# An attention pipeline with a lag of 11 slots in place of 13, and the softmax of a group in three slots in place of five

## What is computed

```
Xq = (H @ W_lin.T).reshape(bt, n, h, dh)
Xv = (H @ W_val.T).reshape(bt, n, h, dh)
Qs = Xq[:, src]
Kt = Xq[:, dst]
e = jnp.einsum('behd,hd->beh', jax.nn.leaky_relu(Qs + Kt, LRELU_SLOPE), a)
e = e + jnp.log(A0[src, dst] + EPS)[None, :, None]
...
attn = ex / denom[src]
Vt = Xv[:, dst].transpose(1, 0, 2, 3)
Y = jax.ops.segment_sum(attn[..., None] * Vt, src, num_segments=n)
...
x = _layernorm(x + _L1_gnn_ref(x, ...))
```

## Time and profile before

| | |
|---|---|
| median of 3 runs | 858.69 us (858.43 to 860.77) |
| the profiled execution | 858.85 us, its span on the core 856.9 us |
| granted TensorE clock, mean | 0.99 |
| PE, DVE, ACT, POOL busy | 822.7, 672.7, 602.1, 262.7 us |
| first weighting of a leaving tile (L1687) | at 662.6 us |
| last weighting of a leaving tile | at 842.2 us |

### The profile page before, as it was taken

The page is one execution under the profiler, slowest core; times in us unless marked ns, Lnnn a source line. Parts: engine busy times, 40 slices in busy tenths (PEclk is TensorE's granted clock), DMA queues, the critical chain, the costliest instruction groups (busy, mean ns, idle before and its releaser), DMA issues.

```text
span 856.9 us, 14362 instructions
## 1 busy us (share of the span) xinstructions
PE 822.7 (96%) x4882; PEld 704.7 (82%) x4882; DVE 672.7 (78%) x1492; ACT 602.1 (70%) x1061; POOL 262.7 (31%) x642
## 2 busy tenths in 40 slices
PE   8999999999999999999999999999999999999685
PEld 7888888878888878888887888878888998988674
DVE  6888888868888878777778677767867787887776
ACT  3778778886767867777666667566787778786345
POOL 0233333340000000000000000102677677777856
PEclk9999999999999999999999999999999999999888
DMA  5222221000000001000000077677248746544513
GB/s 150 63 67 62 63 62 50 2 1 1 2 0 1 1 1 50 1 0 1 1 1 1 0 172 172 147 178 166 99 126 266 232 135 204 173 161 152 176 59 95
DMA packets 37896, 70.55 MB, mean 82 GB/s; under 512 B 3360, under 2 KB 24512, under 8 KB 32704
## 3 DMA queue, kind: packets, MB, share of 16 engines
q0 software_dynamic: 4608, 33.56, 15.3%
q1 hardware_dynamic: 32288, 35.73, 13.3%
q10 hardware_dynamic: 928, 0.35, 0.2%
HBM read 36.06 MB, written 16.78 MB: 62 GB/s over the span
## 4 chain that ended last, share of the span: by engine, by line
PE 77%; POOL 7%; DVE 7%; ACT 4%; issue 3%; DMA 1%; POOLq 0%; DVEq 0%; ACTq 0%
PE psum L514 9%; PE psum L515 9%; PE psum L516 9%; PE psum L532 7%; PE psum L528 6%; PE psum L529 6%; PE psum L424 3%; PE psum L466 3%; PE psum L1406 3%; PE psum L401 2%; PE psum L399 2%; PE psum L400 2%; POOL rstd L1257 2%; PE psum L1329 2%; PE psum L1351 1%
## 5 line engine op out<-in xcount | busy, mean ns | idle before, releaser
L654 ACT ACTIVATE work<-psum,bias 128x512 f32<-128x512 f32 (+2 forms) x364 | 228.9, 666 | 35.8 <-PE psum L532 31.9
L514 PE MATMUL psum<-hT_hi,w_hi 128*128 128x512 f32 (+2 forms) x362 | 139.4, 385 | 1.2 <-ACT work L654 1.2
L515 PE MATMUL psum<-hT_lo,w_hi 128*128 128x512 f32 (+2 forms) x362 | 139.1, 384 | 0.0
L516 PE MATMUL psum<-hT_hi,w_lo 128*128 128x512 f32 (+2 forms) x362 | 138.8, 384 | 0.0
L635 ACT ACTIVATE work<-work 128x512 f32<-128x512 f32 (+1 forms) x100 | 61.3, 613 | 94.8 <-DVE work L977 58.6
L1218 POOL DMA_DIRECT2D hT_lo<-hT_hi x8 | 7.6, 947 | 339.8 <-DVE hT_lo L924 320.4
L988 DVE TENSOR_TENSOR work<-work 128x512 f32<-128x512 f32 (+1 forms) x99 | 66.6, 673 | 47.7 <-ACT work L635 47.7
L528 PE MATMUL psum<-hs_hi,w_hi 128*128 128x512 f32 (+2 forms) x256 | 98.2, 384 | 0.3 <-DVE hs_hi L922 0.3
L532 PE MATMUL psum<-hs_lo,w_hi 128*128 128x512 f32 (+2 forms) x256 | 98.4, 384 | 0.0
L529 PE MATMUL psum<-hs_hi,w_lo 128*128 128x512 f32 (+2 forms) x256 | 97.6, 381 | 0.0
L970 DVE TENSOR_TENSOR work<-work 128x512 f32<-128x512 f32 (+1 forms) x100 | 66.3, 663 | 20.7 <-ACT work L654 20.6
(11 more groups left out here) (234 smaller groups left out, 1888.6 us busy)
## 6 DMA issues: line engine op xcount, KB each, us to landing
work<-x_by_batch SPq DMA_DIRECT2D x32, 256.0 KB, 2.6
x_stage<-x_by_state SPq DMA_DIRECT2D x8, 1024.0 KB, 5.7
hT_lo<-hT_hi POOLq DMA_DIRECT2D x8, 1024.0 KB, 8.4
hT_lo<-x_stage POOLq DMA_DIRECT2D x8, 1024.0 KB, 7.2
v_rows<-values SPq DMA_DIRECT2D x32, 256.0 KB, 2.4
out<-x_kept SPq DMA_DIRECT2D x31, 256.0 KB, 2.4
work<-L_gnn_Wih SPq DMA_DIRECT2D x4, 256.0 KB, 3.0
work<-L_gnn_Whh SPq DMA_DIRECT2D x3, 256.0 KB, 3.2
```

The lines of the kernel that those rows point to most:

```text
L514: pe.matmul(out, w_hi[:, w, g, :], xh, start=True, stop=False)
L515: pe.matmul(out, w_hi[:, w, g, :], xl, start=False, stop=False)
L516: mm = pe.matmul(out, w_lo[:, w, g, :], xh, start=False, stop=(t == 0))
L654: op = act.activation(gate[s][g][:, 0:ph.width(tile)], psum[:, 4 * s + g, 0:ph.width(tile)], ACT.Tanh if g == G else ACT.Sigmoid, bias=bia ...
```

## The change

LAG becomes GT + 3 = 11, RING stays 26 tiles, and the nine steps of the softmax stand in three slots. The exponential stands in the second of them instead of the third. Everything else follows from LAG: slots 0 to 10 take tiles in, slots 11 to 31 do both, slots 32 to 43 bring tiles out; VectorE scales the queries of 11 tiles instead of 13; the late tiles are 21 to 31 instead of 19 to 31. The slots of `LATE_SUMS`, of the value fetches and of the last input load are numbers of their own and stay.

```
@@ -1031,8 +1031,8 @@
-    LAG = GT + 5
-    RING = LAG + 13
+    LAG = GT + 3
+    RING = LAG + 15
@@ -1164,7 +1164,8 @@
-    STEPS = (((0,), (1,)), ((2,), (3,)), ((4,), (5,)), ((6,), ()), ((7,), (8,)))
+    STEPS = (((0,), (1, 2, 3)), ((), (4, 5)), ((6, 7), (8,)))
+    EXP_PART = 1
@@ -1573,7 +1574,7 @@
             g, part = softmax_at(n)
-            if part == 2:
+            if part == EXP_PART:
                 exponentials(g)
```

## The result

| | before | after |
|---|---|---|
| median of 20 runs each, on the same chips | 859.31 us | 861.29 us |
| lowest and highest | 856.07 to 860.95 | 860.51 to 864.55 |
| profiled execution | 858.85, span 856.9 | 861.23, span 859.4 |
| granted TensorE clock, mean | 0.99 | 0.988 |

The ratio is 1.0023 by the medians and 1.0030 by the comparison of the runs, with a 95% interval of 1.0019 to 1.0041: the change costs 2 to 2.6 us, at the edge of what a measurement can tell. The time lies inside the predicted range of 855.6 to 861.9 and 2.6 us above the predicted 858.7.

What follows compares the result with a forecast made beforehand. TensorE was taken to bound the kernel through slot 31, then VectorE until the last softmax is out. Terms 5.36 - 6.22 - 0.72 + 0.90 + 0.50 = -0.18 on 858.85 gave 858.7 us, range 855.6 to 861.9.

Steps and rivals of the forecast that it cites:

- The two regimes: TensorE bounds the kernel until slot 31 ends, then VectorE until the last softmax is out; two leaving tiles move between them.
- 5.36 - 0.72: Slots 11 and 12 become double, +5.36 us; waits around the first leaving tile change by 0.55 + 0.85 - 2.12 = -0.72.
- the 1.41: TensorE's longest wait around the first leaving tile, held up by GpSimd's value fetches; 0 to 1.41 us expected in slot 12.
- Rival 5: Values of the first tiles arrive late; three us of lateness in slot 11 would give 861.7 us; chance 0.02.
- Slots 16 to 31: New TensorE waits: +0.90 us in slot 16 from GpSimd's DMA issues, +0.50 in group 1 from VectorE's moved steps.
- group 2: VectorE's lateness there runs into slot 28's existing 1.09 us wait: put at 0, at most 1.0 us.
- The tail term: Two tiles fewer inside the last softmax on VectorE, 3.11 us each, bring its product earlier by the whole 6.22 us.
- The signs: Product ends some 12 us behind first step; slot 32 about 6 later; waits in slots 9, 12, 16, 20, not 13.
- Rival 1: TensorE's clock doesn't fall after the 4.24 us hole in the tail, saving 3.2: 855.5 us; chance 0.12.
- Rivals 2 to 4: Number 4 here: one more scan holds GpSimd in each of groups 0, 1 and 2, 3 x 0.68: 860.7 us; chance 0.05.
- rival 2: VectorE and GpSimd become the bound during each softmax; all waits at upper bounds, together 3.2: 861.9 us; chance 0.18.
- rival 3: The new waits of 0.55, 0.85, 0.90 and 0.50 don't appear: 855.9 us; chance 0.08.

Runs made afterwards that it cites:

- Experiments 4: Changed kernel with the last group's two accumulating DMAs issued one slot later, in slots 15 and 19: 859.75 us, ratio 1.0000 to the kernel before.
- experiment 5: Changed kernel with each softmax's subtraction moved one slot later, ahead of that slot's weighting: 861.60 us, ratio 1.0025 to the kernel before.
- experiment 3: Both kernels with matmuls on constants filling the tail's TensorE holes: 856.87 us for the changed kernel, 855.92 for the one before.
- experiment 6: Both kernels with tile 22's output issued ahead of the last softmax's turning: 854.60 us for the changed kernel, 853.31 for the one before.

## Why the prediction was right, and where it was off

**The two regimes** held: the price is TensorE's, ahead of slot 32, the gain is VectorE's, behind it, and they nearly cancel. From slot 8's gather to the start of slot 16 it came out as forecast, +4.64 for 5.36 - 0.72, but by luck, with terms that err against each other: slot 9 waits 0.70 instead of 0.55, slot 12 not at all instead of 0.85, and the waits of 0.50 and 0.21, which I let go with the 1.41, only moved to slots 11 and 12. Rival 5 didn't occur: the first weighting waited for no DMA.

**Slots 16 to 31** were mis-sized: 1.40 forecast, 2.58 measured. By the starts of the slots, slot 16 grew by 1.37 (I took 0.90 between 0 and 1.56) and slot 17 by 0.76 (0.50); both are more than the waits of 1.05 and 0.43 that the timeline shows, since matmuls that start after a wait overlap with none before them (slot 16's gather, where it doesn't wait, begins 0.16 us before the matmuls ahead of it end). The rest is mostly group 2, which I put at 0: the lateness of slots 24 and 25 (+1.05) isn't swallowed by slot 28, whose wait shrinks by only 0.53. Experiments 4 and 5 confirm who is late: GpSimd in slot 16, VectorE's moved steps, for the most part, in 9, 17 and 25.

**The tail term** was right in mechanism and off in size: -4.59 instead of -6.22. The failing step is the sentence that TensorE has less to do than VectorE there "in either version, so the product, and all that follows it, comes earlier by the whole 6.22". In microseconds of work that is so. But the two scans and the subtraction that now stand ahead of VectorE's addition make TensorE wait for it, the clock falls in the work behind that hole, and at the lower level TensorE is late for VectorE's next addition. With the holes filled the term is 6.07 (experiment 3), and the product starts 11.67 us behind the first step; with the clock up by itself it is 5.94 (experiment 6).

**The signs** that the prediction named came out mixed. The product ends 13.58 us behind the first step, not some 12; slot 32 begins 7.16 later, not about 6. TensorE waits for the query's low part in slots 9, 16 and 20, not in 12, and not in 13. And one sign of being wrong came: from the start of slot 24 to the end of slot 28 the change adds 1.01 us, more than a turned softmax (0.65 in slot 19). That is the term of group 2, put at 0.

**Rival 1**, that the clock might not fall behind the hole ahead of the turning, didn't come: in all five profiles that have this hole at 4.2 us or more and unfilled, the sum behind it took 3.1 to 3.8 us. Behind shorter holes it is a matter of the single execution: 2.20 and 2.21 ahead of the sum of tile 22 (the result and experiment 6), and in experiment 5 the sum of tile 24 took 2.05 us behind the same hole of 3.20 behind which it took 3.47 to 3.78 elsewhere:

```profile
823.91 2.05 PE L1407 MATMUL psum<-from_node,values 128*128 128x128 f32 x16 [3.20 <-DVE values L1688]
```

That the Trainium skill, page TensorE: Matmul & The Clock Gate, section "Part 1: The HAM clock gate", calls the window free-running fits this; no run here moved that phase on purpose. **Rivals 2 to 4:** the time stands nearer to rival 2's 861.9 than to the forecast, but only 1.18 of its 3.2 us came about, in slots 16 to 31; of the waits that rival 3 leaves out, those of slots 9, 16 and 17 appeared and that of slot 12 didn't; and a scan's hold on GpSimd was seen again (a cast at 689.43 took 0.64 us beside the scan from 689.39) but not tried by itself.

Together the time lies inside the range because two terms that were off in the same direction stayed small: +1.18 in slots 16 to 31 and +1.63 in the tail, with -0.25 for the rest and what lies outside the span. These are the 2.56 between the forecast -0.18 and the 2.38 that the two profiled executions are apart.

## What to carry to other kernels

When work moves between engines, look not only at who is busier in each stretch, but at where the other engine will stand idle in the new order: an idle TensorE can be paid for again in the work that follows. When a schedule shifts, look also at the slots that were left as plain numbers: moving two DMA issues of GpSimd by one slot took away the change's whole loss. Before trading tiles between a stretch bound by one engine and a stretch bound by another, look there for an order that makes both wait for each other; here one output issued ahead of a transposition was worth 6.5 us, and the trade nothing. And where TensorE's clock falls in one version's holes, fill the holes of both with matmuls on constants and compare them so: what is left is the change itself.

## What the runs showed of the hardware

- Behind the same wait the clock fell in one execution and not in another. Behind a wait of 1.64 us in slot 20 the changed kernel ran on at 1.00; behind 1.65 us at the same place, in experiment 5, the clock was granted at 0.63 for four microseconds, and the stretch to slot 24's wait took 29.10 us instead of 27.51. The rows, of the changed kernel and of the kernel of experiment 5:

```profile
716.50:720.50 4.00, 3.91 (x33) 3.91 (x34) 3.05 (x10) 3.56 (x9) 3.31 (x8) 1.00 0.98 318
```

```profile
719.00:723.00 4.00, 3.88 (x21) 3.88 (x22) 2.46 (x8) 2.96 (x6) 3.34 (x8) 0.63 0.95 312
```

- So a wait can cost its own length, or its length and some 1.6 us more. That is most of the difference between the two kernels, and may be a reason why a kernel's runs scatter over 4 us; no run shows that.
- 128x128 matmuls on constants, into a bank that nobody reads, held the clock at 1.00 through holes of 2 to 4 us (798 to 826 in the changed kernel of experiment 3). Where they fitted they cost nothing that the trace shows: the product starts 11.67 us behind the first step with them and 11.81 with the clock up without them. 28 instructions took 3.29 us, more than the hole of 2.20, and delayed the sum by some 0.7.
